# GpSimd takes four weight subtractions of the first block, the next tokens' moments move ahead of the recurrence, and features move in two places

## What is computed

```python
xn = layernorm(x)
q, k, v = (silu(conv4(xn @ W)) for W in (Wq, Wk, Wv))      # q, k normalised by head
beta, g = sigmoid(xn @ Wb), -exp(A_log) * softplus(xn @ Wa + dt_bias)
# per token and head: S = S*exp(g); delta = (v - k@S)*beta; S = S + outer(k, delta); o = q@S
o = o * rsqrt(mean(o*o) + eps) * norm_weight * silu(xn @ Wg)
y = x + o @ Wo + (silu(xn @ gate_w.T) * (xn @ up_w.T)) @ down_w.T   # gate_w, up_w, down_w: splines
```

## Time and profile before

| | |
|---|---|
| three runs, median | 807.68 us |
| three runs, each | 807.45, 812.63, 807.68 us |
| profiled execution, its own time | 812.1 us |
| its span, first to last instruction | 810.3 us |
| PE busy | 759.3 us (94%) |
| DVE busy | 580.9 us (72%) |
| ACT busy | 468.6 us (58%) |
| POOL busy | 357.5 us (44%) |
| chain that ended last, by engine | PE 70%, DVE 20%, issue 4%, ACT 4%, POOL 1%, DMA 1% |

### The profile page before, as it was taken

The page is one execution under the profiler, slowest core; times in us unless marked ns, Lnnn a source line. Parts: engine busy times, 40 slices in busy tenths (PEclk is TensorE's granted clock), DMA queues, the critical chain, the costliest instruction groups (busy, mean ns, idle before and its releaser), DMA issues.

```text
span 810.3 us, 15480 instructions
## 1 busy us (share of the span) xinstructions
PE 759.3 (94%) x5688; PEld 448.3 (55%) x5688; DVE 580.9 (72%) x1403; ACT 468.6 (58%) x1082; POOL 357.5 (44%) x393
## 2 busy tenths in 40 slices
PE   2979599999999999999899999999899999999998
PEld 1456267656657665656674656755344444444443
DVE  5789957878998979998978998577764544545320
ACT  3777835675795766796765687666643333333310
POOL 5148966675894653784663678123330000000000
PEclk9999958999999999999999999999999999999999
DMA  7420041140003022003022001168954414304111
GB/s 216 140 91 18 0 111 40 51 149 12 31 5 124 23 93 79 27 0 126 14 104 80 27 1 34 62 197 179 207 177 104 118 39 104 92 14 111 45 37 42
DMA packets 56113, 63.26 MB, mean 78 GB/s; under 512 B 18375, under 2 KB 41276, under 8 KB 56038
## 3 DMA queue, kind: packets, MB, share of 16 engines
q1 hardware_dynamic: 49430, 45.50, 20.0%
q0 software_dynamic: 4224, 13.11, 5.6%
q10 hardware_dynamic: 2384, 3.67, 1.3%
HBM read 33.69 MB, written 19.73 MB: 66 GB/s over the span
## 4 chain that ended last, share of the span: by engine, by line
PE 70%; DVE 20%; issue 4%; ACT 4%; POOL 1%; DMA 1%; DVEq 0%; POOLq 0%; ACTq 0%
PE bank L672 22%; PE pd L2121 7%; PE pd L2120 7%; PE pd L2119 7%; DVE bank L1213 3%; DVE inv L1219 3%; PE bank L768 2%; DVE cv L1115 2%; PE bank L916 2%; PE bank L861 2%; PE bank L839 2%; PE bank L892 2%; PE bank L759 2%; PE pu L2101 2%; PE pu L2102 2%
## 5 line engine op out<-in xcount | busy, mean ns | idle before, releaser
L672 PE MATMUL bank<-x_parts,w 128*128 128x512 f16 x576 | 137.0, 385 | 1.8 <-DVE x_parts L1072 1.5
L2188 DVE TENSOR_TENSOR hh<-sg,pu 128x512 f32<-128x512 f32 x64 | 43.9, 687 | 96.1 <-ACT sg L2158 91.2
L672 PEld LDWEIGHTS bank<-x_parts,w 128*128 128x128 f16 x576 | 59.4, 106 | 63.8 <-issue 6.8
L2066 POOL DMA_DIRECT2D yr<-y_attn x16 | 8.8, 552 | 181.8 <-DMA out<-yr 181.8
L672 PE MATMUL bank<-w,x_parts 128*128 128x384 f16 x384 | 80.9, 343 | 6.6 <-DVE inv L1219 6.6
L2158 ACT ACTIVATE sg<-pg 128x512 f32<-128x512 f32 x64 | 38.0, 595 | 71.0 <-PE pg L2102 71.0
L1115 DVE SCALAR_TENSOR_TENSOR cv<-raw,taps,cv 128x512 f32<-128x512 f32 x72 | 56.1, 829 | 0.6
L672 PEld LDWEIGHTS bank<-w,x_parts 128*128 128x128 f16 x384 | 37.0, 110 | 26.3 <-DVE inv L1219 7.4
L1739 POOL TENSOR_TENSOR rn<-t,mhalf 128x6 f32<-128x6 f32 x16 | 22.8, 1422 | 65.2 <-DVE t L1305 65.2
L1213 DVE TENSOR_TENSOR bank<-bank,inv 128x60 f32<-128x60 f32 (+32 forms) x184 | 47.1, 285 | 2.2
L2119 PE MATMUL pd<-dw,it 128*128 128x512 f16 x128 | 48.5, 379 | 0.0
(11 more groups left out here) (302 smaller groups left out, 2064.2 us busy)
## 6 DMA issues: line engine op xcount, KB each, us to landing
xr<-in_x SPq DMA_DIRECT2D x16, 256.0 KB, 2.6
y_attn<-xr SPq DMA_DIRECT2D x16, 256.0 KB
down_rows<-inv SPq DMA_DIRECT2D x8, 512.0 KB, 4.3
yr<-y_attn POOLq DMA_DIRECT2D x16, 256.0 KB, 3.0
out<-yr SPq DMA_DIRECT2D x16, 256.0 KB, 3.1
xb<-in_x SPq DMA_DIRECT2D x3, 1024.0 KB, 5.6
xn_hi<-x_parts POOLq DMA_DIRECT2D x4, 512.0 KB
xn_lo<-x_parts POOLq DMA_DIRECT2D x4, 512.0 KB
```

The source lines that it names most:

```text
L672: ins = nc.tensor.matmul(out, a, b, start=first and i == 0, stop=last and i == 2)
L2188: v.tensor_tensor(hh[:, i % 2, :], sg[:, i % 2, :], pu[i % 2][:], ALU.mult).then_inc(h_ready, 1)
```

## The change

In the first block, ACT first scales a staged piece in place (float32 to float32), waits for that, and then copies it to the high part, for pieces 4 to 7. GpSimd then makes the low part as a plain difference (`scaled_low`): for piece 4 behind the edges of block 3, for 5 behind the third `masked_g`, for 6 and 7 behind the root `nk`. DVE makes none of these four. `scores` of chunks 0 and 2 wait for the low parts of pieces 4 and 5. ACT's high part of piece 5 stands before the last two silus of the keys and queries. GpSimd's four `mask_weights` of the first block stand behind the placing of the inverses (L1813 before) and ahead of the cubics.

`ln_moments` stands in `solve`, behind the last statistics and ahead of the last copy into `W`, in the three blocks that have a following one.

In the last block's chunk 3, PE makes features 2 and 3 behind `project_out`, and `transpose_out` stands ahead of the wait for their low parts; DVE's `feature_lo` 2 and 3 stand behind gating and residual; ACT's `og_high` stands ahead of `downs.first`. In `feed`, for the first 512 tokens alone, the following block's four features stand behind groups 6 to 9 and not 4 to 7.

```diff
 def piece_high(self, act, i):
+        if i >= NSTG:
+            self.nc.scalar.activation(src, src, ACT.Copy, scale=scale).then_inc(self.scaled, 1)
+            act.wait_ge(self.scaled, i - NSTG + 1)
+            scale = 1.0
         self.nc.scalar.activation(hi, src, ACT.Copy, scale=scale).then_inc(self.hi_done, 1)
...
+    def scaled_low(self, pool, i):
+        pool.wait_ge(self.hi_done, self.count(i))
+        pool.wait_ge(self.lo_done, self.count(i) - 1)
+        src, hi, lo = self.parts(i)
+        self.nc.gpsimd.tensor_tensor(out=lo, in0=src, in1=hi, op=ALU.subtract).then_inc(self.lo_done, 1)
...
             def scores(s, c):
+                if s.first() and c % 2 == 0:
+                    dve.wait_ge(prep.lo_done, prep.count(NSTG + c // 2))
...
                         ln_tile_stats(following, STATS_IN[k])
+                        if k == NCH + 2:
+                            ln_moments(following)
...
-                    if s.first() and c < NSTG - 1:
-                        prep.piece_low(dve, NSTG + 1 + c)
...
-                if following is not None and c == 0:
-                    ln_moments(following)
...
-            prep.piece_low(dve, NSTG)
...
                 gates(s, 0, 1)
+                if s.first():
+                    prep.piece_high(act, NSTG + 1)
                 silu(s, NQK - 2)
...
+                    if n == NPAIR and s.first():
+                        prep.scaled_low(pool, NSTG)
                 masked_g(s, 1)
...
                     masked_g(s, c)
+                    if s.first() and c == 2:
+                        prep.scaled_low(pool, NSTG + 1)
...
-                for c in range(NCH - 1):
-                    mask_weights(s, c)
+                if s.first():
+                    for i in range(NSTG + 2, 2 * NSTG):
+                        prep.scaled_low(pool, i)
+                else:
+                    for c in range(NCH - 1):
+                        mask_weights(s, c)
...
                 if s.first():
+                    for c in range(NCH):
+                        mask_weights(s, c)
                     pool.wait_ge(samples.ctrl_in, 48)
```

The features of the last block and of `feed` (PE; DVE and ACT are moved likewise):

```diff
                 else:
+                    project_out(s, c - 2)
                     if c == NCH - 1 and s.idx() == nst - 1:
                         start.features(pe, s0, 2, bank[0])
                         start.features(pe, s0, 3, bank[1])
-                    project_out(s, c - 2)
...
                 if c == NCH - 1 and s.idx() == nst - 1:
+                    transpose_out(s, c - 1)
                     pe.wait_ge(start.feat_lo, 4)
...
-                    if following is not None and 6 <= n < 6 + HB:
-                        start.features(pe, following, n - 6, pf[n % 2])
+                    if following is not None and 6 <= i < 6 + HB:
+                        start.features(pe, following, i - 6, pf[i % 2])
```

More of the change, by code:

```diff
@@ L901, in recur @@
                 if c >= 2:
-                    transpose_out(s, c - 1)
+                    if not (c == NCH - 1 and s.idx() == nst - 1):
+                        transpose_out(s, c - 1)
                     state_products(s, c, "QS", 1)
@@ L1367, in recur @@
                     start.turned_low(dve, 0, bank[0])
-                if b.idx() == nst - 1 and c == NCH - 1:
-                    start.feature_lo(dve, s0, 2, bank[0])
-                    start.feature_lo(dve, s0, 3, bank[1])
                 if following is not None and c in (1, 2):
@@ L1378, in recur @@
                     residual(b, c - 2)
+                if b.idx() == nst - 1 and c == NCH - 1:
+                    start.feature_lo(dve, s0, 2, bank[0])
+                    start.feature_lo(dve, s0, 3, bank[1])
+                if c >= 2:
                     og_part(b, c - 1)
@@ L1512, in v_tokens @@
                     act.wait_ge(nk_ready, s.val(1, 1))
+                if n == 0 and s.first():
+                    act.wait_ge(prep.lo_done, prep.count(2 * NSTG - 1))
                 for c in range(NCH):
@@ L1597, in local @@
                         take_diagonals(s, c - 1)
-                    if s.first() and c < NSTG - 1:
+                    if s.first() and 1 <= c < NSTG - 1:
                         prep.piece_high(act, NSTG + 1 + c)
@@ L1667, in recur @@
                 updates(b, c)
+                ahead = c == NCH - 1 and b.idx() == nst - 1
+                if ahead:
+                    og_high(b, c - 1)
                 downs.first(act, NCH * b.idx() + c, SCRATCH)
-                if c >= 2:
+                if c >= 2 and not ahead:
                     og_high(b, c - 1)
@@ L2168, in groups @@
                         start.feature_hi(act, s, HB + n, pf[n % 2])
-                    if following is not None and 6 <= n < 6 + HB:
-                        start.feature_hi(act, following, n - 6, pf[n % 2])
+                    if following is not None and 6 <= i - 1 < 6 + HB:
+                        start.feature_hi(act, following, i - 7, pf[(i - 1) % 2])
                     gated(s, i)
@@ L2212, in groups @@
                         start.feature_lo(dve, s, HB + n, pf[n % 2])
-                    if following is not None and 6 <= n < 6 + HB:
-                        start.feature_lo(dve, following, n - 6, pf[n % 2])
+                    if following is not None and 6 <= i - 1 < 6 + HB:
+                        start.feature_lo(dve, following, i - 7, pf[(i - 1) % 2])
                 inter_lo(s, IB - 1)
```

11 lines of the change are left out of this document (6 added, 5 removed).

## The result

The changed kernel took 812.56 us (median of 20 executions, 810.69 to 816.9) against 809.34 us of the kernel before, measured beside it (20 executions, 805.88 to 812.79). The ratio is 1.004, with a 95% interval of 1.0025 to 1.0055: some 3.2 us slower. Comparisons here leave disturbed executions out, so a ratio can differ from that of two medians beside it.

A forecast was written before the change was run, and what follows sets the result against it. DVE was taken to bound the kernel before 101 us unless ScalarE is late, PE the feed-forward part. Seven terms summed to +2.75 us on a median of 807.68, giving 810.4 us; range 803.5 to 816.

The forecast's parts named there:

- two collisions and a clock as before: Likeliest case: both GpSimd low parts hold DVE's convolution steps, clock unchanged; 810.4 us, chance 0.52.
- GpSimd late at the recurrence: First block: four masks ahead of the cubics delay them 5.7 us, idle time absorbs 5.4; +0.3 us (0 to 1.5).
- low clock gone: Rival: in the first block's assembly, half or all of 10.1 us is won; 805.4 or 800.3 us, chance 0.10.
- Second low part: Piece 5 on GpSimd holds DVE's last two fused convolution steps of blocks 4 and 5; +3.6 us (0 to 3.8).
- First low part: Piece 4 on GpSimd holds DVE's convolution at about 35 us, delaying block 2's silu; +1.65 us (0 to 3.3).
- DVE's return: First block's scores: four low parts, over 8 us, leave DVE, but ScalarE becomes the bound; -0.3 us (-2 to +1).
- Moments: Steps moved into `solve`: +1.1 us in the first block, net -1.2 in the second and third each; sum -1.3.
- Last recurrence: Last block: PE's 1.36 us wait before features 2 and 3 goes, 1.2 us idle comes at the polynomial; -0.3 us.
- Feed-forward part: PE's 1.93 us wait at a moved feature shrinks as two features leave groups 4 and 5; -0.9 us (-2 to 0).
- The rival without any collision: GpSimd steps need not hold DVE for their whole length in the convolution; 805.2 us, chance 0.12.

The follow-up runs named there:

- the masks late alone: Kernel before with only GpSimd's four first-block masks moved behind the placing of the inverses, ahead of the cubics: 1.0065 of before.
- the GpSimd part alone: Kernel before with only scaling in place, four low parts on GpSimd and masks behind the placing; moments, last recurrence and feed-forward as before: 1.0071 of before.
- without the GpSimd part: Changed kernel with low parts on DVE, no scaling in place, masks where they were: 0.9952 of before, 0.9955 in a second set.
- masks in the gaps: Changed kernel with the first mask behind the edges of block 6, two behind the last taps, the fourth behind the first `rn`: 1.0033 of before.
- the changed kernel again: The changed kernel unaltered, measured once more against the kernel before: 1.0013 of before.
- `rn` amid the cubics: Changed kernel with GpSimd making `rstd` and the first `rn` between the two halves of the cubics: 1.0103 of before.
- the moments alone: Kernel before with only `ln_moments` moved into the assembly: 0.9948 of before.

## Why the prediction came out as it did

I gave +2.75 us; it is +3.2 (2.0 to 4.5). The sum is near by luck; its terms are not. One that I put at 0.3 was the largest, one that I put at 3.6 comes in some executions only, and the fast assembly that hid the first was a rival to which I gave 0.10 and quite other times. The story that I held likeliest, two collisions and a clock as before, is not what the profiled execution shows.

- **GpSimd late at the recurrence, +0.3 (0 to 1.5): the step that failed.** Measured 5.3 us alone, 6.6 to 6.8 at full clock. The delay of 5.7 us was right (116.35 for 110.57). What failed is the slack that I took off it: the 3.65 us of idle time ahead of `rn`, read from an execution whose assembly took 29.9 us. With an assembly of 22 us there is none, and the 5.8 us come through. I had the case "low clock gone" as a rival of its own (805.4 or 800.3) and did not ask what it does to the other terms: in it the backlog comes alive, and GpSimd keeps the clock's gain. The executions say so too: with the masks late, those at the higher clock are at most 2.8 us faster than those at the lower one (811.8 for 812.6 and 811.3 for 813.1 in the changed kernel, 815.8 for 815.5 with the masks late alone, 814.2 for 817.0 with the GpSimd part alone, where only three are at the higher), where it is 5.0 us before (809.2 for 814.2) and 10.2 without the GpSimd part (803.6 for 813.8).
- **Second low part, +3.6.** It meets the convolution in three traces (GpSimd's part alone, masks in the gaps, the changed kernel again), as I had it, and adds 2.8 us to the 6.48 of before (9.32), not 3.6. In these PE's clock was 1.00 from 42 to 48 us. In the four others with this order it was 0.56 to 0.72 there, and the low part came too late to meet them; ScalarE's earlier high part stands ahead of the last silus instead. I argued from ScalarE's end at 49.1, which holds only with PE at 2.4 GHz.
- **First low part, +1.65.** In every trace that has it DVE's scaling took 3.26 us. 1.1 us at the silu, since a low part takes 3.10 us. My price of 3.6, and its lower bound of 3.3, were too high: 1024 columns more than the 1.43 us row of 512 cost 1.67 us, where I took 2.2 from another form. The Trainium skill's figure (GPSIMD Engine Reference, Elementwise side-by-side cycle accounting), from which the estimate was 3.3, was nearer.
- **DVE's return, -0.3.** As said: 8 us leave DVE, and the last scores wait 2.67 us for ScalarE. After's inversion began 1.2 us later than before, so both collisions' terms and this one come to +1.2 there, where I had +4.95. In the two traces of this order with the second collision that kept the masks out of the spline they come to 3.2 and 3.4 at T1 (start differences taken off), and in that with `rn` amid the cubics to -0.3. 4.95 was met in none.
- **Moments, -1.3.** 1.3 us net in the second block (I said 1.2): all eleven traces with the moved moments take 125.9 to 126.5 us from T2 to T3, the three without 127.4 to 127.5. In the first I said +1.1: beside the cubics the steps did take 2.6 us and PE waited 1.57 us, but gating waits for GpSimd in any case, and the moments alone won 3.3 to 4.2 us. The step counted a loss on an engine that ends early there. From T2 to T4 its trace takes 2.6 us less than that of before; what the rest of the 3.3 is was not traced, since no execution of before with a fast assembly was profiled.
- **Last recurrence, -0.3.** PE was 0.15 us later than in before when it began (511.43 for 511.28) and 0.15 earlier when it ended (565.66 for 565.81): -0.3, with the new wait at the polynomial (0.91 for 1.2). From T4 to the feed-forward part the four traces with the old order take 72.7 us, the ten with the new one 72.3 to 72.4.
- **Feed-forward part, -0.9.** From 0.15 us ahead at its start to 0.9 at the end of the span: -0.75. One pair does not settle this: two executions of the kernel without the GpSimd part differ by 2.4 us in this stage alone (242.9 and 245.3), and the kernels with the old order took 243.8 to 246.0. The term is not shown by itself.

The rival without any collision stands refuted for streaming steps: in the places shown, where GpSimd streamed through SBUF when DVE's step came, DVE's ended with it. The Trainium skill (SBUF — State Buffer, Who interferes with whom) says of the shared ports that who comes first holds them for the whole instruction; the traces agree for the low part (3.26 us for 0.48), the masks (1.90 for 0.28) and the taps (1.25 for 0.28), and not for the root of 24 columns, beside which a low part took 1.80 us.

The best versions are the change without its GpSimd part, 0.9952 and 0.9955 of before in two sets, some 3.8 us less than before and 7 less than the changed kernel, and the moments alone (0.9948). Their intervals overlap; at the higher clock the first is 2 us or more ahead (803.6 and 804.0 for 806.0), of which the earlier start may be 1.3.

## What to carry to other kernels

A slack that is read from one execution belongs to the clock of that execution: where a stage has run slowly in the trace, work out every term that leans on its length a second time with the stage at full speed. A step put on an idle engine is paid for by all that stands behind it in that queue, and on GpSimd also by each small SBUF step that DVE makes beside it. Before moving work to free DVE, look which engine ends the wait next: here it was ScalarE, which the move had loaded as well.

## What was unexpected in the hardware

Behind the same gap at the end of the inversion, with PE idle from 96 to 99 us in both, PE's clock stayed at 1.2 GHz until past 126 us in the profiled execution of before and was back at 2.4 GHz by 105 in that of after. Windows of after and before:

```profile
102.00:105.00 3.00, 3.00 (x30) 1.45 (x30) 3.00 (x2) 1.69 (x2) 0.00 (x0) 0.64 0.85 312
105.00:108.00 3.00, 3.00 (x87) 2.29 (x81) 2.55 (x7) 2.15 (x6) 2.61 (x4) 1.00 0.45 104
```

```profile
102.00:105.00 3.00, 3.00 (x11) 1.22 (x8) 3.00 (x2) 1.59 (x2) 0.10 (x1) 0.50 0.87 324
105.00:108.00 3.00, 3.00 (x55) 2.34 (x55) 1.91 (x6) 1.10 (x3) 2.56 (x3) 0.50 0.37 85
```

It is no property of the edit: the changed kernel had its assembly at 0.93 in one trace and at 0.58 in another. In after the clock had fallen by 99 us already (0.73 from 96 to 99, for 1.00). The other traces bear this out. By the mean clocks of windows of 1 us (an estimate to some 0.1 us), it fell 1.1 to 1.4 us ahead of T1 in the three traces with a slow assembly, and came back only some 26 us behind T1; in the eleven others it fell 1.6 to 7.2 us ahead and came back 3.0 to 5.2 us behind. In before, with the masks late and with the moments alone PE had stood idle equally long (6.3 us), and the fall came 1.3, 1.6 and 1.8 us ahead. So the clock came back soon where it had fallen a little sooner. That the earlier fall is the cause, and what sets its moment, was not tried and stays open. The assembly alone differs by 8 us, more than any part of this change.
